# Attention of a gated cross-attention block reordered: double-buffered x rows and value tiles, earlier x steps, probability transposes issued ahead

## The reference

```python
x = x + tanh(g_xattn[0]) * xattn(layernorm(x), ctx)
x = x + tanh(g_ffn[0]) * ffn(layernorm(x))

def xattn(x1, x2):                       # x1: 16 x 512 x 512, x2: 16 x 77 x 512
    q, k, v = x1 @ Wq.T + bq, x2 @ Wk.T + bk, x2 @ Wv.T + bv      # 16 heads of 32
    attn = softmax(einsum('bhnd,bhmd->bhnm', q, k) / sqrt(32))
    return einsum('bhnm,bhmd->bhnd', attn, v) @ Wo.T + bo         # heads joined again

def ffn(x):                              # 512 -> 2048 -> 512
    hidden = x @ W1 + b1
    imag = w_imag * sin(theta + hidden * 0.1)
    q = hidden + (cos(theta) * w_real + sin(theta) * w_imag) * imag * 0.1
    return relu(q) @ W2 + b2
```

## Time and profile before

| | |
|---|---|
| median of 3 runs | 2297.01 us |
| profiled execution, own time | 2293.67 us |
| its span (first to last instruction) | 2291.9 us |
| PE / weight loads / DVE / ACT / POOL busy | 94 / 75 / 64 / 49 / 18% |
| granted PE clock, mean over the span | 0.97 |
| DRAM and SBUF traffic | 79 GB/s, 383938 packets, 305760 of them under 512 B |
| SP's block moves into xT | 256 transfers of 64 KB, 2.3 us from issue to landing |

### The profile page before, as it was taken

How to read it: one execution, slowest core, us unless ns; L and a number is a source line. 1 busy time by engine, 2 the same in 40 slices (tenths; PEclk the granted TensorE clock), 3 DMA queues, 4 the chain that set the end, 5 groups by cost and what they waited for, 6 DMA issues and landing times.

```text
span 2291.9 us, 29183 instructions
## 1 busy us (share of the span) xinstructions
PE 2143.9 (94%) x10321; PEld 1718.9 (75%) x10321; DVE 1457.4 (64%) x2521; ACT 1130.3 (49%) x3399; POOL 408.8 (18%) x331
## 2 busy tenths in 40 slices
PE   8877888887888889999999999999999999999999
PEld 7765566665666666788888888888888888888887
DVE  4566666675666665866666666665665665665654
ACT  3365455555555553644444444444444444444443
POOL 3032333332333333010010110110110110110110
PEclk9999899998999999999999999999999999999999
DMA  7434334434334443431231231231232221221210
GB/s 210 149 58 107 93 89 97 101 85 112 98 88 96 98 107 126 125 74 56 55 74 55 56 74 56 51 76 58 39 80 64 39 74 57 54 72 48 65 37 19
DMA packets 383938, 181.89 MB, mean 79 GB/s; under 512 B 305760, under 2 KB 320522, under 8 KB 383793
## 3 DMA queue, kind: packets, MB, share of 16 engines
q1 hardware_dynamic: 382433, 179.52, 31.2%
q0 software_dynamic: 928, 0.48, 0.1%
q10 hardware_dynamic: 432, 0.04, 0.0%
HBM read 106.34 MB, written 56.85 MB: 71 GB/s over the span
## 4 chain that ended last, share of the span: by engine, by line
PE 59%; DVE 1%; ACT 0%; issue 0%; ACTq 0%; DVEq 0%
PE pair_bank L56 30%; PE m_bank L56 30%; DVE w_split L1404 0%; DVE hidden L1438 0%; DVE turns L1434 0%; DVE sine L1431 0%; ACT relu L1364 0%; ACT hidden L1373 0%; ACT turns L1375 0%; DVE stats L180 0%; DVE relu L1421 0%; DVE x_in L205 0%; ACT sine L1380 0%; DVE residual L1446 0%; DVE mean L190 0%
## 5 line engine op out<-in xcount | busy, mean ns | idle before, releaser
L56 PE MATMUL pair_bank<-w_split,relu 128*128 128x512 f32 x3072 | 738.3, 389 | 3.9 <-DVE relu L1421 3.2
L56 PE MATMUL m_bank<-xT,w_split 128*128 128x512 f32 x3024 | 726.4, 389 | 0.0
L56 PEld LDWEIGHTS pair_bank<-w_split,relu 128*128 128x128 f32 x3072 | 576.5, 188 | 125.2 <-issue 3.6
L56 PEld LDWEIGHTS m_bank<-xT,w_split 128*128 128x128 f32 x3024 | 567.6, 188 | 117.7
L1032 ACT ACTIVATE exps<-pair_bank,lowest 128x77 f32<-128x77 f32 x1024 | 317.1, 350 | 205.8 <-DVE lowest L1075 205.8
L1380 ACT ACTIVATE sine<-turns 128x512 f32<-128x512 f32 x256 | 161.8, 632 | 393.6 <-DVE turns L1434 393.6
L1364 ACT ACTIVATE relu<-hidden 128x512 fp32r<-128x512 f32 x256 | 161.9, 632 | 330.8 <-PE m_bank L56 231.7
L1421 DVE SCALAR_TENSOR_TENSOR relu<-hidden,relu 128x512 fp32r<-128x512 f32 x256 | 181.2, 708 | 202.1 <-ACT relu L1364 202.1
L1438 DVE SCALAR_TENSOR_TENSOR hidden<-sine,sine_gain,hidden 128x512 f32<-128x512 f32 x256 | 196.9, 769 | 169.8 <-ACT sine L1380 169.8
L200 POOL TENSOR_TENSOR rstd<-var_eps,minus_half 128x4 f32<-128x4 f32 x32 | 38.2, 1194 | 1152.8 <-DVE var_eps L196 1152.8
L1032 ACT ACTIVATION_READ_ACCUMULATOR exps<-pair_bank,lowest 128x1 f32 x1024 | 237.5, 232 | 0.0
(11 more groups left out here) (120 smaller groups left out, 1819.4 us busy)
## 6 DMA issues: line engine op xcount, KB each, us to landing
x_in<-in_x_dram SPq DMA_DIRECT2D x16, 1024.0 KB, 5.5
residual<-in_x_dram SPq DMA_DIRECT2D x64, 256.0 KB, 2.9
xT<-x_in SPq DMA_DIRECT2D x256, 64.0 KB, 2.3
x_scratch<-residual SPq DMA_DIRECT2D x64, 256.0 KB, 2.3
x_in<-x_scratch SPq DMA_DIRECT2D x16, 1024.0 KB, 5.5
residual<-x_scratch SPq DMA_DIRECT2D x64, 256.0 KB, 3.6
out_dram<-residual SPq DMA_DIRECT2D x64, 256.0 KB, 2.1
quad_scratch<-x_in SPq DMA_DIRECT2D x60, 256.0 KB, 5.1
```

The lines of the kernel that those rows point to most:

```text
L56: mm = pe.matmul(out, stationary(s), moving(m), start=first and n == 0, stop=last and n == len(PASSES) - 1)
```

## The change

It touches attention and the end of setup.

- **x rows**: a second buffer x_odd; batch b lies in x_rows[b % 2]. The load of batch b+3 stands at the head of SP's slot 2, sums and statistics in slot 3, normalise in slot 0 and turn_rows in slot 2 (half each side of queries_lo), moves in slot 3 behind the first scores, x_hi in slot 0, x_lo in slot 1. Batch 1's rows are summed, normalised and turned in setup.
- **values**: v_diag has two buffers, written at batch b for b+1 in slot 2; 12 transfers a batch as before, in rows of 256 bytes (v_sum is stored with the two groups of a head side by side). **Keys**: loaded for two groups at once, 8 transfers a batch instead of 16.
- **transposes**: chunks 0 and 1 of the next pair go on PE between output and value products of an odd slot, chunk 2 into the even slot behind the queries, chunks 3 and 4 to the head of the next odd slot. The last two are copied to probsT by ACT in place of DVE.
- **values products** begin when the first of their banks is free; the second bank is waited for only before the second step. DVE's heads_lo of the second group moves into the next slot.
- **the end**: the last four outputs use the four banks of pair_bank in place of the two of m_bank, and the slots are one list for all engines.
- POOL's gating of bo moves from the start to batch 1.

```diff
-        v_diag = sb(att, "v_diag", [P, 2, G // 2, NC, P])
+        v_diag = [sb(att, f"v_diag{i}", [P, 2, NC, HG, 2 * DH]) for i in range(2)]
+        x_odd = sb(att, "x_odd", [P, NT, D])
+        x_rows = [x_in, x_odd]
...
+        def load_keys(queue, b, pair, loaded):
             for j in range(HG):
                 rows = slice(j * DH, (j + 1) * DH)
+                queue.dma_start(k_diag[rows, 2 * pair:2 * pair + 2, :, j * M:(j + 1) * M].rearrange("p g s m -> p (g s) m")
+                                .bitcast(F32),
+                                k_parts[b, rows, 2 * pair:2 * pair + 2].rearrange("p g s m -> p (g s) m"))\
                   .then_inc(loaded, 16)
...
+        def load_values(queue, b, loaded):
+            for second in range(2):
+                for j, c, p0, m0, n in pieces[second]:
+                    h = HG * second + j
+                    queue.dma_start(v_diag[b % 2][p0:p0 + n, second, c, j, :],
+                                    v_rows_all[bass.ds(M * b + m0, n), 2 * DH * h:2 * DH * (h + 1)]).then_inc(loaded, 16)
...
@@ setup, vector @@
-                    for j in range(RT):
-                        values_sum(ROUNDS - 1, j)
+                    sums(dve, 2, x_odd)
+                    values_sum(ROUNDS - 1, 0)
+                    statistics(dve, 2)
+                    values_sum(ROUNDS - 1, 1)
+                    normalise(dve, 2, x_odd)
+                    values_sum(ROUNDS - 1, 2)
...
+                    turn_rows(dve, 1, range(NT))
                     hidden_constants()
@@ attention, sync @@
+                def load_x(b):
+                    for moved in blocks_moved:
+                        sp.wait_ge(moved, 16 * QUADS * (b - 2))
+                    sp.dma_start(x_rows[b % 2][:, :, :], x_tiles[b] if b < B else x1_tiles[b - B]).then_inc(x_loaded, 16)
...
+                for s in slots:
+                    b, g = s.b, s.g
+                    if g == 2:
+                        if b + 3 <= B:
+                            load_x(b + 3)
...
+                        if b + 1 < B:
+                            if b >= 1:
+                                sp.wait_ge(m_full, values_of[2 * b - 1][1][0])
+                            load_values(sp, b + 1, values_loaded[(b + 1) % 2])
+                    if g == 3 and b + 2 <= B:
+                        sp.wait_ge(scores_full, 2 * G * b + 2 * g + 1)
+                        move_blocks(b + 2)
+                    if g == 3 and b >= 1:
+                        reload_residual(b, 0)
+                    if g < 3 and b >= 2:
+                        reload_residual(b - 1, g + 1)
+                    if s.odd and b + 1 < B:
+                        sp.wait_ge(scores_full, 2 * G * b + 2 * g + 2)
+                        load_keys(sp, b + 1, g // 2, keys_loaded[g // 2])
+                    if s.output:
+                        store_y(*s.output[:3])
@@ attention, gpsimd @@
+                    if g == 0 and 1 <= b and b + 2 <= B:
+                        rstd_of(pool, b + 3)
...
+                    if b >= 1:
+                        add_bias(b - 1, g)
+                    if s.score:
+                        probabilities(2 * G * b + 2 * g + 1, g, 0)
+                        probabilities(2 * G * b + 2 * g + 2, g, 1)
@@ attention, tensor @@
+                    pe.wait_ge(m_split, values[0][0] - 2)
                     for step in range(len(strips[0])):
+                        if step == 1:
+                            pe.wait_ge(m_split, values[1][0] - 2)
...
+                        if s.odd and s.pair is not None:
+                            for c in LATE_C:
+                                transpose_probs(s.pair, c)
+                        for half in range(2):
+                            scores(b, g, half, s.queries_done)
+                        if s.queries:
+                            queries(b + (g == 3), (g + 1) % G, *s.queries[:2])
+                        if not s.odd and s.pair is not None:
+                            transpose_probs(s.pair, NC - 1)
                         if s.output:
+                            block_output(*s.output)
+                        if s.next_pair is not None:
+                            for c in range(NC - 1):
+                                transpose_probs(s.next_pair, c)
+                    if s.values:
+                        value_products(s.pair, s.values)
@@ attention, scalar @@
+                    if s.odd and s.pair is not None:
+                        copy_late_probs(s.pair)
+                    if s.score:
+                        exponentials(2 * G * b + 2 * g + 1, 0)
+                    if s.queries:
+                        queries_hi((g + 1) % G, *s.queries[:2])
+                    if s.score:
+                        exponentials(2 * G * b + 2 * g + 2, 1)
+                    if (b == 0 and g == 1) or (1 <= b < B and g == 0):
+                        x_hi(b + 1)
+                    if s.values:
+                        for second in range(2):
+                            heads_hi(s.pair, second, *s.values[second][:2])
@@ attention, vector @@
+                    if s.score:
+                        peaks(unit + 1, 0)
+                    if s.earlier_values:
+                        heads_lo(s.pair - 1, 1, *s.earlier_values[1][1:])
+                    if s.score:
+                        peaks(unit + 2, 1)
+                    if not s.odd:
+                        if s.pair is not None:
+                            for c in range(NC - 1):
+                                copy_probs(s.pair, c)
                         if s.score:
                             inverse(unit + 1, 0)
+                        if g == 0 and 1 <= b and b + 2 <= B:
+                            normalise(dve, b + 3, x_rows[b % 2], range(HALF))
+                        if g == 2 and b + 2 <= B:
+                            turn_rows(dve, b + 2, range(HALF))
+                        if s.pair is not None:
+                            copy_probs(s.pair, NC - 1)
+                    else:
+                        if g == 1 and 1 <= b < B:
+                            x_lo(b + 1, range(NT))
+                        if g == 3 and b + 3 <= B:
+                            sums(dve, b + 4, x_rows[(b + 3) % 2])
                         if s.score:
+                            inverse(unit + 1, 0)
+                    if s.queries:
+                        queries_lo((g + 1) % G, *s.queries[1:])
...
+                    if g == 3 and b + 3 <= B:
+                        statistics(dve, b + 4)
+                    if s.output:
+                        gate_output(*s.output[:3], m_bank[s.output[3]])
+                    if s.score:
+                        inverse(unit + 2, 1)
+                    if s.values:
+                        heads_lo(s.pair, 0, *s.values[0][1:])
```

More of the change, by code:

```diff
@@ L174, in gated_attention_ffn_kernel, with sums @@
         normed = sem(whole, "normed")
-        def sums(dve, n, tiles=range(NT)):
+        def sums(dve, n, rows, tiles=range(NT)):
             dve.wait_ge(x_loaded, 16 * n)
             for tile in tiles:
-                dve.bn_stats(stats[:, tile, :], x_in[:, tile, :]).then_inc(stats_ready, 1)
+                dve.bn_stats(stats[:, tile, :], rows[:, tile, :]).then_inc(stats_ready, 1)
         def statistics(dve, n):
@@ L802, in scores_view, with transposed @@
+            slots, outputs_after = slots_of()
+            values_of = {s.pair: s.values for s in slots if s.values}
+            def transposed(pair, c):
+                n = PC * pair + c + 1
+                return n, (n - 1) % 2
             def scores_view(half):
@@ L1024, in x_hi @@
+                def x_hi(b):
+                    for moved in blocks_moved:
+                        act.wait_ge(moved, 16 * QUADS * b)
+                    for tile in range(NT):
+                        act.activation(xT[b % 2][0][:, tile, :], xT[b % 2][1][:, tile, :].bitcast(F32),
                                        ACT.Copy).then_inc(x_hi_ready, 1)
@@ new lines, in _ @@
+                    if b == 0 and g == 0:
+                        sums(dve, 3, x_rows[0])
+                        statistics(dve, 3)
+                    if b == 0 and g == 1:
+                        normalise(dve, 3, x_rows[0])
+                    if b == 0 and g == 2:
+                        x_lo(1, range(NT))
+                    if not s.odd:
+                        if g == 0 and 1 <= b and b + 2 <= B:
+                            normalise(dve, b + 3, x_rows[b % 2], range(HALF, NT))
+                        if g == 2 and b + 2 <= B:
+                            turn_rows(dve, b + 2, range(HALF, NT))
@@ new lines, in _ @@
+                    if g == 3 and b + 3 <= B:
[6 more added lines that the diff above has]
+                        heads_lo(s.pair, 0, *s.values[0][1:])
+                dve_last = slots[-1]
+                heads_lo(dve_last.pair, 1, *dve_last.values[1][1:])
+                for tile, n, _ in outputs_after:
```

(1 more changed line is left out.)

427 lines of the change are left out of this document (153 added, 274 removed).

## The result

The changed kernel takes 2147.54 us (median of 4 runs, 2146.75 to 2149.03), beside 2296.65 us of the kernel before on the same chip (4 runs, 2295.5 to 2299.79): ratio 0.935, 95% interval 0.9333 to 0.9366. The profiled execution took 2147.3 us, its span 2145.5.

What follows compares the result with a forecast made beforehand. PE bounds the kernel, held in attention by a late x load through DVE's order. Fourteen batches' gain of 132.6, less 7.0 stalls, plus 11 and 2, gives 138.6: 2155.1 from the profiled execution, 2158 us as median; range 2143 to 2199.

Steps and rivals of the forecast that it cites:

- The floor and the holes: Steady attention batches: PE's work alone takes 39.2 us against 48.5, once the late x_in load no longer delays qT.
- The allowance for stalls: Steady batches: 0.5 us of remaining PE waits taken per batch, 7.0 in all, from bounds of 0 to 2.3.
- The cover of slot 1: DVE in slot 1: qT done at 7.6 us, PE's values ask at 8.9, about 1.2 us of cover.
- The step that called the even slot overfull: DVE's even slot: about 8.7 us of work against PE's 7.7; the odd slot's 7.5 of 11.7 covers the overhang.
- The 0.94 us wait: PE's wait for the gated residual ahead of values products: goes, with 0.1 to 0.3 us left per pair.
- Head and tail: Batches 0 and 1 with setup gain 11 us (bounds 0 and 18); the last outputs gain 2 (-2 to +3).
- DVE against POOL: Slot 1's x_lo: clashes of 1.1 us; two further ones cost about 1 us a batch, 14 in all, giving 2172.
- A: Rival: a chain of DVE and ACT sets the pace, a batch takes 41.5 us, 2183 to 2198 us; chance 0.22.
- B: Rival: SP's queue sets the pace, 2 to 5 us a batch, 2185 to 2225 us; chance 0.07.
- C: Rival: DVE's sums still wait for the x load, nothing is gained, 2290 to 2301 us; chance 0.03.
- D: Rival: slower; moves landing over 12.3 us late hold ACT's x_hi in slot 0, 3 us slack; chance 0.03.

Runs made afterwards that it cites:

- experiment 1: Changed kernel with the x load moved to the head of SP's slot 3 (first kernel, 2206.03 us) or behind that slot's sixteen moves (second, 2367.32 us).
- experiment 2: Kernel before, with only the x load moved on SP's queue, to slot 1 just before the value loads; one buffer, old order elsewhere: 2226.76 us, ratio 0.9712.
- experiment 5: Changed kernel with one, three or five further bn_stats into an unread buffer on DVE in slot 1, behind x_lo: 2148.57, 2158.8 and 2178.32 us.
- experiment 4: Changed kernel with the two late probsT copies put back from ACT to DVE, at the head of the odd slot: 2151.45 us, ratio 0.9376.
- experiment 3: Changed kernel with the next pair's two transposes behind the values products instead of between output and products: 2151.15 us, ratio 0.9379.
- experiment 7: Changed kernel with one key load per group again and value rows of two 128-byte pieces: 2153.18 us, ratio 0.938.
- experiment 6: Changed kernel with slot 3's 16 block moves behind that slot's residual load, key loads and store: 2166.75 us, ratio 0.9439.

## Why the prediction was right

- **The floor and the holes.** 14 x 39.2 less 2.8, or 546.0, was forecast and 546.09 measured; values products of 2.78 us throughout. The reading that PE was held by a load through DVE's order is shown by experiments 1 and 2: load later, and the hole is back; load earlier in the old kernel, and it is gone.
- **The allowance for stalls** (7.0 us) is the term that was mis-sized: it measured 0, and is 7.0 of the 10.5 us by which the forecast was too high. Of the rest, 0.9 are head and tail, and some 3 are the step from one execution to the median: 3.3 before, 0.2 after (2147.54 beside 2147.3). The cover of slot 1 was walked as 1.2 us and is 1.6; the added work of experiment 5 shows it within 0.2. The range's low end, 2143, was said to be the sum with no stalls and 15 for the head; that sum is 2147.4 with the 3.3 us carried, 2144.1 without. No stalls is what happened, so 2147.54 lies where the forecast's own low end should have stood.
- **ACT** came out at 29.1 us a batch (29.5 forecast), **DVE** at 30.6 (29.5). The 1.1 us that the forecast lacks are for the most part normalise's, where it saw no clash:

```profile
L205 DVE TENSOR_SCALAR x_in<-x_in,mean,rstd 128x512 f32<-128x512 f32 x56 | 26.7, 538 | 0.0
L205 DVE TENSOR_SCALAR x_in<-x_in,mean,rstd 128x512 f32<-128x512 f32 x28 | 23.5, 878 | 0.0
```

  The first row is of the kernel before, the second of the changed one, both over the fourteen batches (in the changed one 24 more, of x_odd, took 19.2 us): 16 us more in all. In the changed kernel some of the four in a batch took up to 1.6 us, as the one at 413.63, beside POOL's bias add (413.43 to 414.88). The step that called the even slot overfull, with its overhang covered, holds: DVE was given two more copies a pair in experiment 4 and PE did not wait.
- **SP** was forecast at 30 us of 39 and is at 23: the values were charged the old 10.0 us and took 4.2, and keys of twice the bytes took 1.86 where 2.5 was kept. A cost of nothing in the sum, so nothing was lost by it; with the old transfers it is 33.7, and still nearly off the path.
- **The 0.94 us wait** goes, and the 0.1 to 0.3 us left for it did not show. It was put down to two causes, the transposes ahead and the relaxed bank wait. Experiment 3 shows that the transposes are not needed for it, to 0.1 us, which leaves the second; that one was not undone alone.
- **Head and tail.** 11 and 2 were taken, 12.0 and 1.9 measured. But the head was right by luck, of two errors that nearly cancel: setup's end cost 4.1 us and not 2.5, and batches 0 and 1 gained 16.1.
- **DVE against POOL.** In the changed kernel the slowest of the 64 x_lo took 1816 ns beside a median of 680, so a clash of up to 1.1 us remains, about one a batch. The Trainium skill (SBUF — State Buffer, "SBUF: two separate sides") has the two lock each other out for a whole instruction; the trace agrees in size, and experiment 4, where x_lo fell to 680 ns throughout, shows that it hangs on where the two happen to lie. The 2172 us that followed from the rule needed two further clashes in front of qT. The further clashes came in slot 0, in normalise, and none ate up the 1.6 us of slot 1.
- **The rivals.** A needed DVE to exceed its cover: it takes 1.6 us more in slot 1 for that (experiment 5). B falls with experiment 7. C did not happen; the second kernel of experiment 1 is what it looks like. D's place was right: experiment 6 shows that late moves reach PE there, and that 7.5 us later costs 1.3 us a batch. D's own reckoning, 3 us of slack and all beyond it on PE's path, would have made it 4.5; so it priced a late move too high, at least at this size. 12.3 us later was not tried.
- **What each step gave**, as far as shown: of 149 us by the medians, the place of the x load alone 66 (4.8 of a batch's 9.3); the rest comes from what takes sums, copies and gate out of PE's way. In the new order the copies on ACT (experiment 4) and the transposes ahead (experiment 3) are worth 0 and less than 0.1 us a batch. The second x buffer, DVE's new order and the relaxed bank wait were not undone, so how the other half splits stays open.

## What to carry to other kernels

Find the wait that ends last in front of the bounding engine, then follow the waiting engine's own order back to the transfer that holds it: here one load, queued behind 12 small ones, was worth nearly half of what a large reordering brought. When covers are walked, check the thinnest by adding dummy work of known size at that point; three kernels measured it to 0.2 us. And look where the moved work lands: the end of setup gave at least 4 us back for two moved lines.

## What the runs showed of the hardware

- **Issue time did not go by bytes.** Twelve value loads took 10.0 us to issue as two pieces of 128 bytes a row, 4.2 as one of 256, the same bytes. Key loads took 0.47 us each with one group (eight in 3.73) and with two (four in 1.86), though 0.62 at the place of the earlier trace rows. So fewer pieces a row helped the values, and twice the pieces a row cost the keys nothing.
- **A 1 MB load** landed 5.3 to 5.7 us after its issue in the kernel before. With sixteen moves queued right behind it (the first kernel of experiment 1) it took 5.6 to 6.3 us in twelve of fourteen cases, 7.0 and 8.0 in the others.
- **The same hole does not always cost the clock.** Behind equal holes of 2.31 us in the kernel of experiment 2, by windows over the values products:

```profile
398.78:401.56 2.78, 2.78 (x25) 0.85 (x26) 2.63 (x11) 2.12 (x11) 1.87 (x3) 1.00 0.29 107
441.27:445.74 4.47, 4.47 (x25) 1.20 (x26) 2.70 (x11) 2.11 (x11) 3.56 (x4) 0.62 0.43 129
```

  The granted clock stayed at its upper level (2.4 GHz) in one product and fell, for most of the product, to its lower one (1.2 GHz) in the other; between 202 and 600 us it fell behind six of nine such holes. Holes of 0.2 to 2.0 us cost no clock in the steady batches of experiment 5. But in the first kernel of experiment 1, where a hole of 1.6 to 2.3 us for qT was followed, 1.06 us of products later, by one of 0.9 for the gate, the clock fell in eight of twelve batches.
